# The last block of a relative-position attention layer, finished in halves, with its transfers and rows in another order

## The reference

```python
xn = layernorm(x)
q, k, v = heads(xn @ Wq.T + bq), heads(xn @ Wk.T + bk), heads(xn @ Wv.T + bv)
idx = clip(key - query, -128, 128) + 128           # 256 x 256
scores = (q @ k.T + q . rel_k[idx]) / sqrt(8)
w = softmax(scores)
att = w @ v + w . rel_v[idx]                       # content part + relative part
x + (att @ Wo.T + bo) + ffn(xn)                    # ffn: two layers with ternary weights
```

## Time and profile before

| | before |
|---|---|
| median of 3 runs | 478.08 us |
| the profiled execution's own time | 478.54 us |
| its span | 476.7 us |
| PE / DVE / ACT / POOL busy | 88% / 85% / 87% / 66% |
| granted TensorE clock, mean | 0.97 |

### The profile page before, as it was taken

How to read it: one execution, slowest core, us unless ns; L and a number is a source line. 1 busy time by engine, 2 the same in 40 slices (tenths; PEclk the granted TensorE clock), 3 DMA queues, 4 the chain that set the end, 5 groups by cost and what they waited for, 6 DMA issues and landing times.

```text
span 476.7 us, 24894 instructions
## 1 busy us (share of the span) xinstructions
PE 417.7 (88%) x10258; PEld 337.7 (71%) x10258; DVE 406.0 (85%) x881; ACT 416.6 (87%) x806; POOL 313.5 (66%) x370
## 2 busy tenths in 40 slices
PE   0788888679999999999999999999999999999733
PEld 0345554577888887888888888888888888887622
DVE  8879766469989999999999899999999999999535
ACT  2879999469999999999999999999999999999300
POOL 6547777527574777768687768777686868775400
PEclk9989999999999999999999999999999999999955
DMA  7623745952104443424243334515242425522694
GB/s 167 221 53 111 126 89 136 168 127 69 37 27 83 72 67 71 94 43 87 55 78 73 66 67 82 96 38 92 49 82 58 71 62 93 89 55 52 119 261 130
DMA packets 159464, 43.09 MB, mean 90 GB/s; under 512 B 122256, under 2 KB 156536, under 8 KB 159224
## 3 DMA queue, kind: packets, MB, share of 16 engines
q1 hardware_dynamic: 154352, 40.45, 41.6%
q10 hardware_dynamic: 5000, 1.05, 1.3%
HBM read 21.55 MB, written 16.79 MB: 80 GB/s over the span
## 4 chain that ended last, share of the span: by engine, by line
PE 50%; issue 12%; ACT 9%; DVE 7%; DMA 1%; SPq 1%; ACTq 0%; DVEq 0%
PE ps_s L1019 10%; PE ps_s L1014 9%; PE ps_s L1116 9%; PE ps_o L1036 9%; PE ps_t L1101 7%; DVE mx L1225 5%; PE ps_r L1060 4%; ACT xr L1153 4%; ACT big L1188 4%; ACT p L1168 1%; PE ps_s L1091 1%; SPq L933 1%; DVE big L1229 1%; DMA xr<-rel_dram 1%; DMA rel_dram<-xr 1%
## 5 line engine op out<-in xcount | busy, mean ns | idle before, releaser
L860 POOL TENSOR_TENSOR big<-p,big 128x512 f16<-128x512 f32 x128 | 148.6, 1161 | 101.7 <-ACT big L1188 101.0
L1019 PE MATMUL ps_s<-by_q_room,e 96*128 96x64 f16 x2048 | 103.1, 192 | 0.0
L1014 PE MATMUL ps_s<-qbd,kst 96*128 96x128 f16 x1024 | 99.5, 219 | 3.1 <-PEq L300 2.5
L1229 DVE TENSOR_TENSOR big<-ps_y,big 128x512 f16<-128x512 f32 x128 | 88.0, 687 | 15.3 <-ACT big L1188 13.8
L1266 DVE TENSOR_REDUCE mcol<-ps_t 128x4 bf16<-128x512 bf16 x128 | 87.5, 684 | 9.0 <-PE ps_t L1101 5.3
L1225 DVE TENSOR_TENSOR mx<-s,ps_s 128x512 bf16<-128x512 bf16 x128 | 86.6, 676 | 3.2 <-ACT s L1146 2.1
L1146 ACT ACTIVATE s<-ps_s 128x512 bf16<-128x512 f32 x128 | 80.2, 627 | 6.0 <-PE ps_s L1019 5.9
L1019 PEld LDWEIGHTS ps_s<-by_q_room,e 96*128 96x128 f16 x2048 | 85.4, 97 | 0.0
L1188 ACT ACTIVATE big<-p 128x512 f16<-128x512 f32 x128 | 84.6, 661 | 0.0
L1168 ACT ACTIVATE ps_y<-ps_s 128x512 f32<-128x512 f32 x128 | 76.0, 593 | 7.5 <-PE ps_s L1116 3.1
L276 POOL COPY by_q_room<-qrel 96x256 uint32<-96x256 uint32 x128 | 78.4, 629 | 3.1 <-POOLq L300 3.1
(11 more groups left out here) (110 smaller groups left out, 523.2 us busy)
## 6 DMA issues: line engine op xcount, KB each, us to landing
rel_dram<-xr SPq DMA_DIRECT2D x32, 256.0 KB, 3.4
xr<-rel_dram SPq DMA_DIRECT2D x64, 128.0 KB, 3.7
kst<-big SPq DMA_DIRECT2D x48, 64.0 KB, 2.0
qrel<-qr_dram SPq DMA_DIRECT2D x192, 16.0 KB
qbd<-q_dram SPq DMA_DIRECT2D x192, 16.0 KB
y_dram<-big SPq DMA_DIRECT2D x4, 512.0 KB, 2.8
big<-y_dram SPq DMA_DIRECT2D x4, 512.0 KB, 6.0
out<-big SPq DMA_DIRECT2D x8, 256.0 KB, 3.4
```

The lines of the kernel that those rows point to most:

```text
L860: nc.gpsimd.tensor_tensor(probs[:, k // 8, 1, 1, k % 8, :], p32[:, k % 2, 1, :], probs[:, k // 8, 0, 1, k % 8, :], ALU.subtract).then_inc( ...
L1014: nc.tensor.matmul(bank[:, P * g:P * g + P], kst[:, g, S * k + P * kh:S * k + P * kh + P], rhs, start=(g == 0), stop=False, skip_group_che ...
L1019: ins = nc.tensor.matmul(bank.rearrange("p (h q j) -> p h q j", q=Q0, j=J)[:, :, q, :], e4[:, first:first + P], rhs.rearrange("p (h j) -> ...
L1229: nc.vector.tensor_tensor(probs[:, k // 8, 1, 0, k % 8, :], ps_y[:, :], probs[:, k // 8, 0, 0, k % 8, :], ALU.subtract).then_inc(lo0_ready, 1)
```

## The change

It touches what stands at the end of the last query block and behind the loop:

1. **Two parts a step.** In the last query block PE computes block 14's relative values two parts a step, in steps 9 to 12. ACT moves its halves in steps 11 and 13.
2. **Rest rows earlier in SP's list.** `load_rest(0)` and `(1)` stand ahead of block 14's load, so that nothing but block 14's second save stands ahead of them; `load_rest(2)` and `(3)` behind it, ahead of block 15's saves.
3. **Block 15: saves first, then loads, by halves, on two queues.** Both saves stand ahead of its loads. `load_last` brings back one half (parts of one move) in four transfers of 64 KB, two issued by SP and two by ACT, with a semaphore for each half (`last_in`). The outputs of part 0 are now written behind them in SP's list.
4. **Finishing by halves.** `finish_half` takes two reciprocals, two additions and a multiplication over half of a block, twice for block 14 and for block 15. `last_ready` counts to 4; `project(2)` waits for 2, `project(3)` for 4.
5. **DVE's order.** `add_rest(0)` goes behind the mask and sum of the last unit; `add_rest(2)` stands between the two halves of block 15.

```diff
+            if qb == NQB - 1 and k in (first - 2, first):
+                return qb, 0, (k - first + 2) // 2
...
+        def load_last(eng, half, groups):
+            m = BG * NQB - 1
+            eng.wait_ge(rel_out[half], 16 * (m + 1))
+            for g in groups:
+                src = rel_dram[m, g, half].rearrange("j (y d) (h n) -> (d h) j y n", d=HD, h=HH)
+                eng.dma_start(land[32 * g:32 * g + 32, m % 2, 4 * half:4 * half + 4, :, :], src).then_inc(last_in[half], 16)
...
             save_relative(last - 1, 0)
             save_relative(last - 1, 1)
             load_rest(0)
+            load_rest(1)
             load_relative(last - 1)
-            load_rest(1)
-            save_relative(last, 0)
             load_rest(2)
             load_rest(3)
-            save_relative(last, 1)
-            save_out(0, 0)
-            save_out(0, 1)
-            load_relative(last)
-            for m in range(1, len(OUT_PARTS)):
+            for half in range(2):
+                save_relative(last, half)
+            sp.wait_ge(att_ready, last - 1)
+            for half in range(2):
+                load_last(sp, half, range(0, 2))
+            for m in range(len(OUT_PARTS)):
                 for half in range(2):
                     save_out(m, half)
...
+                if qb == NQB - 1 and 9 <= k < 13:
+                    relative(qb, 0, 2 * (k - 9))
+                    relative(qb, 0, 2 * (k - 9) + 1)
...
-                wait(pe, last_ready, (0, 1 + bg)[qh])
+                wait(pe, last_ready, (0, 2 + 2 * bg)[qh])
...
-            relative(NQB - 1, 0, len(REL_PARTS) - 1)
             pv(NQB - 1, UNITS - 3)
...
-            move_relative(NQB - 1, 0, 1)
             move_relative(NQB - 1, 1, 0)
             move_relative(NQB - 1, 1, 1)
+            act.wait_ge(att_ready, BG * NQB - 2)
+            for half in range(2):
+                load_last(act, half, range(2, 4))
...
-            def finish_block(m):
+            def finish_half(m, half):
+                done = 2 * (m - (BG * NQB - BG)) + half + 1
+                x = slice(4 * half, 4 * half + 4)
+                sums = block_of_att(m)[:, x]
+                for piece in range(2):
+                    denominators(m, 2 * half + piece)
...
-            add_rest(0)
             own_heads(NQB - 1, UNITS - 1)
             sum_heads(NQB - 1, UNITS - 1)
-            finish_block(BG * NQB - 2)
+            add_rest(0)
+            for half in range(2):
+                finish_half(BG * NQB - 2, half)
             add_rest(1)
-            finish_block(BG * NQB - 1)
+            finish_half(BG * NQB - 1, 0)
             add_rest(2)
+            finish_half(BG * NQB - 1, 1)
             add_rest(3)
```

More of the change, by code:

```diff
@@ L809, in build_main @@
         rrden_ready, att_hi_added, att_lo_added, att_ready = sem("rrden_ready"), sem("att_hi_added"), sem("att_lo_added"), sem("att_ready")
+        last_in = [sem(f"last_in{i}") for i in range(2)]
         last_hi_added, last_lo_added, last_ready = sem("last_hi_added"), sem("last_lo_added"), sem("last_ready")
@@ L826, in relative_of @@
                     at = first + 8 * bg + 4 * half
-                    if k == at % UNITS and (at < UNITS or unit(qb, -1)):
-                        return qb - at // UNITS, bg, half
+                    own = qb - at // UNITS
+                    if k == at % UNITS and own >= 0 and (own, bg) != (NQB - 1, 0):
+                        return own, bg, half
         def block_at(qb, k, first):
@@ L1070, in relative_step @@
                         part = k + UNITS * back - (9 + 8 * bg)
+                        if qb - back == NQB - 1:
+                            continue
                         if 0 <= part < len(REL_PARTS) and not (back and isinstance(qb, int) and qb == 0):
@@ L1250, in denominators @@
             def denominators(m, piece):
+                if m == BG * NQB - 1:
+                    dve.wait_ge(last_in[piece // 2], 16 * G)
+                elif piece == 0:
+                    dve.wait_ge(land_in[m % 2], 16 * LOADS * (m // 2 + 1))
                 if piece == 0:
-                    dve.wait_ge(land_in[m % 2], 16 * LOADS * (m // 2 + 1))
                     wait(dve, att_ready, m - 1)
@@ L1290, in _ @@
             loop(dve, body)
[L1292 to L1296 removed]
+            def finish_half(m, half):
[4 more added lines that the diff above has]
+                    denominators(m, 2 * half + piece)
                 dve.wait_ge(out_summed, 8 * (m + 1))
[L1298 removed]
+                nc.vector.tensor_tensor(sums, sums, landed(m, 0)[:, x], ALU.add).then_inc(last_hi_added, 1)
                 dve.wait_ge(last_hi_added, done)
[L1300 removed]
+                nc.vector.tensor_tensor(sums, sums, landed(m, 2)[:, x], ALU.add).then_inc(last_lo_added, 1)
                 dve.wait_ge(last_lo_added, done)
[L1302 to L1304 removed]
+                dve.wait_ge(rrden_ready, 4 * m + 2 * half + 2)
+                nc.vector.tensor_tensor(sums, sums, reciprocals(m)[:, x], ALU.mult).then_inc(last_ready, 1)
             def add_rest(m):
```

8 lines of the change are left out of this document (removed).

## The result

The changed kernel takes 471.06 us, the median of four executions (469.95 to 472.79), against 477.88 (477.27 to 479.91) for the kernel before in four. The ratio is 0.9853, with a 95% interval of 0.9808 to 0.9899. The profiled execution took 470.23 us and its span is 468.4; forecast were 468.7 and 467.3. It was run once more beside the experiments: 469.91 us (469.33 to 470.4), ratio 0.9835 (0.9819 to 0.985). So the gain is 7 to 8 us where 9.4 was forecast. Among the four executions the profiled one is one of the two fastest; the others reach 472.79.

What follows compares the result with a forecast made beforehand. Behind the loop, block 15's save and load, blocked on SP, were taken to bound the kernel; afterwards DVE's list. `project(3)` at 460.1 plus 7.16 gave span 467.3 against 476.7, time 468.7 us, range 466.0 to 472.5.

Steps and rivals of the forecast that it cites:

- The loop's end: Steps 9 to 15 of the last query block: exponentials of the last unit 0.5 us later, bounds 0 and +1.3.
- Saves issued: SP issues block 15's two saves right after ACT's moves, at 447.2 and 448.9 us.
- Saves landing: Block 15's saves take 3.4 and 3.0 us to land, at 450.7 and 452.0.
- The half loads: Block 15's loads on two queues: 4.0 us from landed save, first half landed at 454.7, second at 456.0.
- DVE: Behind the loop: block 14 done at 452.9, block 15's halves at 456.7 and 460.0, 2.0 us a half.
- No gap over 1 us: Sign expected in the profile after: DVE has no gap over 1 us between 447 and 460.
- Late instructions: Rival, chance 0.08: one stall of 1.4 us for an instruction block on the critical engine gives 470.1 us.
- The tail: From the start of `project(3)` to the span's end: 7.16 us, unchanged, with matmuls at half clock.
- transfers stay last: Rival, chance 0.18: block 15's saves queue behind rest rows, landing in 5.6 us; span 469.3, time 470.7.
- slower than before: Rival, chance 0.03: late instruction blocks in steps 13 to 15 cost 1.4 us each; eight give 479.9 us.
- It does not do what it says: Rival: block 15's halves land together, so DVE's halving only costs 1.1 us, giving 469.8; chance included in 0.18.
- DVE's own range: Likeliest path, DVE's chain, chance 0.58: 466.8 to 470.8 us, from bounds on the loop and each half block.

Runs made afterwards that it cites:

- the control: The changed kernel, unaltered, measured a second time beside the experiments: 469.91 us, ratio 0.9835 to the kernel before.
- part 1 undone: The changed kernel with block 14's relative values one part a step again and its second move behind the loop: 477.66 us, ratio 0.9997.
- SP's order alone: The kernel before with only the end of SP's list reordered, block 15's saves ahead of rest rows 1 to 3: 473.33 us, ratio 0.9911.
- the kernel with fourteen idle matmuls: The changed kernel with 14 matmuls into an unread PSUM bank between `project(2)` and `project(3)`: 472.54 us, ratio 0.9891.
- the one with eight small matmuls more: The changed kernel with eight small f32 matmuls added on PE at the program's start: 472.74 us in its one execution.

## Why the prediction came out as it did

The mechanism was right and the size of the gain was 1.1 us too large in the profiled execution's span (467.3 forecast, 468.4 measured). The medians, 471.06 and 469.91 us, lie 2.4 and 1.2 above the forecast's 468.7. The span's difference is made of these terms.

- **The loop's end.** Forecast +0.5 us, measured 439.87 - 439.53 = +0.34 for the last transposes. A doubled step took 2.82 us, not 2.93. In the control the last transposes came at 440.61, over 1 us later than before: the bound of +1.3 was needed.
- **Saves issued.** Forecast 447.2 and 448.9, measured 448.22 and 450.0. Most of the missing 1.0 us is the first stall, 0.88 us in block 15's first half, where the forecast had none.
- **Saves landing. This is the term that was sized wrong, at 3.4 us for 4.8.** I took "the median 3.4 for the first (450.7) and 3.0 for the second (448.9 + 3.0 = 452.0)"; they took 4.8 and 3.7. The row that fitted was the one I used as a bound, 5.6 us behind two loads of rest rows: here, too, two such loads were in flight, not finished until 451.64. With those two loads moved away the saves took 2.3 and 2.5, with the two doubled 6.7 and 4.9. Together with the later issue the first half landed at 456.95 instead of 454.7.
- **The half loads.** Forecast 4.0 us from the landed save to the landed half, measured 456.95 - 453.07 = 3.9. Right. All eight go out within 2 us, and the last lands by 458.4, some 1.4 us behind the first half (forecast 1.3).
- **DVE.** From the landed half to the end of the second half forecast 460.0 - 454.7 = 5.3 us, measured 462.03 - 456.95 = 5.1. Right. Block 14 done at 452.9, measured 453.5. "No gap over 1 us" held, with 0.81, 0.94 and 0.33, but the first two, for `project(1)`, were not in the sum.
- **Late instructions.** This was a rival with a chance of 0.08 and one stall of 1.41 us. It came twice, 0.88 and 3.03 us (in the control 0.73 in the loop and 1.94), and was the step most underrated: the row was seen and its place known, but its length was carried over as if it were a constant. In `project(1)` it was 0.33, 0.57, 1.11 and 1.11 us in the four variants of the changed kernel that have those rest rows elsewhere, and 1.94 to 3.58 in the profiles of six that have both right ahead of the saves; it was 1.95 and 2.23 where block 14's load was still flowing (part 1 undone, SP's order alone). The Trainium skill (Runtime: NRT & Kernel Launch, "Instruction fetch mechanics") has instructions fetched in 16 KiB blocks by a DMA queue and for the most part unnoticed. The packet of that size in the DMA view, the 254 records between two stalls and the stall that moved by the count of added instructions agree with the blocks, while 3.0 us of standing PE on the critical path is not unnoticed. How late the block comes is seen in the packet: in all 14 profiles it lies 2.1 to 2.8 us ahead of the matmul that ends this stall. With rest rows 2 and 3 moved behind, it went at 446.3, before PE was at the place (448.5), in the changed kernel at 450.5, after PE was (450.0). What passes in the 2 to 3 us between packet and matmul no run shows.
- **The tail.** Forecast 7.16 us from the start of `project(3)`, measured 468.4 - 462.13 = 6.3. The clock, back at full level in the window of 456 to 457 us, fell only at 463.1, so the first microsecond of `project(3)` ran at full clock. This gave back 0.9 us, and it was luck: the forecast did not have it, and in the control it did not happen (468.0 - 460.84 = 7.2, the forecast's term). Why the clock outlasted 4.19 us of standing here and not 3.96 us there is not shown.
- **Sum.** Issue of the saves +1.0, landing +1.4, half loads and DVE -0.3, which gives `project(3)` at 462.13 against 460.1; tail -0.9; span +1.1. Without the tail's luck the forecast would have been 2.0 us short.

The rival "transfers stay last" was the nearest to what happened: the saves queued as it said, though for 4.8 us and not 5.6, and DVE was never kept waiting long. The rival of lost slack in the loop ("slower than before", chance 0.03) did not come in the first profiled execution, but it did in small in others: PE stood 0.73 us in the loop in the control and 0.20 to 0.77 in five variants, and the stretch from step 9 to the last transposes, 16.38 us before, took 17.73 in the control. That is 1.35 us more, just beyond the 1.3 that the prediction had named as a sign of being wrong. "It does not do what it says" was half true: halving block 15 is worth nothing by itself, but does not cost 1.1 us either.

What the parts are worth, by the runs: SP's order from the kernel before 4.4 us; the order as changed needs part 1 and makes nothing without it; halves and the second queue nothing measurable. Two readings of the prediction were slightly off without moving its result: a window with a mean clock of 0.92 puts the fall at 454.84, not 454.92, and DVE's own range begins at 467.1 by its bounds, not 466.8.

Open are the spread between the two measurements of the changed kernel (471.06 and 469.91, intervals overlapping), why the issues of block 14's load take 4 to 6 us where four issues can take 2.3, and the late rest rows of the kernel with fourteen idle matmuls.

## What to carry to other kernels

Check an ordered list of transfers against the time at which each entry's source is ready: an order gains only if what stands ahead of an entry is ready and issued before it. One order gained 4.4 us here by itself; the changed kernel's gained nothing until part 1 made its earlier entries ready in time. Price a transfer by the row that has the same traffic in flight ahead of it, not by the median, and expect bulk transfers to delay the instructions of the busiest engine as well. Where the chain ends in matmuls behind a wait, ask which clock they will get, since an earlier input can be spent on a slower engine.

## What the runs showed of the hardware

- PE stood 0.33 to 3.70 us between two matmuls with no semaphore between them, in all 14 profiles at the same count of instructions. Where a second stall stood ahead of it behind the loop, 127 matmuls and their weight loads lay between. One transfer of 16 KB of the instruction queue lies 2.1 to 2.8 us ahead of the matmul that ends the stall, as well where the stall was 0.33 us as where it was 3.70; the stall is long where that transfer goes late. In nine stretches looked at around these stalls the other queue's share of the DMA engines was 32% and 44% where the stall was 0.33 and 1.11 us, and 71 to 118% where it was 1.94 to 3.70 (and 1.41 in the kernel before).
- A save of 256 KB took 2.3 to 3.1 us with rest rows 2 and 3 out of its way, 2.7 to 5.7 in the kernels that issue these two loads (1 MB) just ahead of the saves, and 6.7 and 4.9 with them doubled.
- The same 16 recorded matmuls of the last projection took 3.75 us at the granted clock of 0.5 and 2.02 at 1.0. How long PE stood just before does not by itself tell which: with 1.03 us the clock was kept, with 1.84 it fell as the projection began, with 3.96 to 5.28 it had fallen before in most profiles, but with 4.19 in the first profile of the changed kernel, and 4.61 in the one with eight small matmuls more, it fell only some 1 and 0.7 us into the projection.
- Four issues of 128 KB on SP took from 2.3 to 6.4 us, by what was in flight; four of 64 KB took 1.9 us and eight of them 4.04, with little in flight.
